# A transformer block in float32: input tiles of the feed forward turned in PSUM banks of their own, and a new order of exponentials, rounding, normalising and splitting in cross attention

## The reference

```
x = x + cross_attention(layernorm(x), ctx)    # 16 heads, queries against a latent context of 257 x 128 per batch
x = x + self_attention(layernorm(x))          # 16 heads of 32
x = x + feed_forward(layernorm(x))
# cross attention, folded, for each batch b (scores of 512 rows = 16 heads x 32 queries):
#   attn = softmax(q_b @ kv_b.T); ctx_c = attn @ kv_b; out = ctx_c through per-head weights
# feed forward:
amp = sigmoid(x @ amp_w + amp_b)
ph  = tanh(x @ ph_w + ph_b) * pi
h   = (cos(ph) + sin(ph)) * amp
for l in range(2):
    h = layer_norm(h + (h @ ent_w[l] + ent_b[l]) @ ent_pw[l] + ent_pb[l], ln3_g[l], ln3_b[l])
    t = einsum('bsd,pdf->pbsf', h, path_w[l]) + path_b[l]
    h = layer_norm(h + sum_p(t * (cos(phase[l]) + sin(phase[l]))), ln4_g[l], ln4_b[l])
```

## Time and profile before

| | |
|---|---|
| median of 3 runs | 1646.76 us (1643.83 to 1646.97) |
| profiled execution | 1646.83 us, its span 1644.8 us |
| mean granted clock of TensorE | 0.956 of full speed |
| cross attention, 600 to 900 us | PE busy 97%, DVE 80%, ACT 53%, POOL 51% |
| feed forward, 1421.8 to 1503.3 us (one turn) | PE busy 94%, DVE 57%, ACT 51%, POOL 25% |

### The profile page before, as it was taken

The page is one execution under the profiler, slowest core; times in us unless marked ns, Lnnn a source line. Parts: engine busy times, 40 slices in busy tenths (PEclk is TensorE's granted clock), DMA queues, the critical chain, the costliest instruction groups (busy, mean ns, idle before and its releaser), DMA issues. The chain is left out here.

```text
span 1644.8 us, 26366 instructions
## 1 busy us (share of the span) xinstructions
PE 1490.0 (91%) x8136; PEld 1129.7 (69%) x8136; DVE 1124.7 (68%) x1815; ACT 809.7 (49%) x1723; POOL 539.5 (33%) x593
## 2 busy tenths in 40 slices
PE   4799999999946999999999987999799499898998
PEld 3577777777635777777777766888444278777876
DVE  6788778887526878787878753777558535555556
ACT  4566665566434555555555533555201355545554
POOL 4235324341024554545454513221051331402021
PEclk9899999999977999999999997999899699999999
DMA  4123334324257544454454414000354000000000
GB/s 152 64 90 95 105 107 127 100 84 114 82 174 242 123 115 116 106 124 109 122 108 116 132 27 168 0 0 1 128 204 154 0 1 1 1 27 0 26 26 26
DMA packets 140505, 143.77 MB, mean 87 GB/s; under 512 B 83488, under 2 KB 103072, under 8 KB 138784
## 3 DMA queue, kind: packets, MB, share of 16 engines
q1 hardware_dynamic: 138720, 133.87, 28.2%
q10 hardware_dynamic: 1728, 9.20, 1.7%
HBM read 113.54 MB, written 29.49 MB: 87 GB/s over the span
## 5 line engine op out<-in xcount | busy, mean ns | idle before, releaser
L942 ACT ACTIVATE c_e_t_high<-c_et_ps 128x512 fp32r<-128x512 f32 x128 | 76.7, 599 | 227.4 <-PE c_et_ps L1011 227.4
L820 POOL TENSOR_TENSOR c_mixed_low<-c_whole,c_mixed_high 128x512 fp32r<-128x512 f32 x64 | 96.0, 1500 | 177.1 <-ACT c_mixed_high L954 177.1
L77 DVE TENSOR_TENSOR b_rot_parts_low<-b_rot,b_rot_parts_high 128x1536 fp32r<-128x1536 f32 x64 | 136.0, 2125 | 21.9 <-ACT b_rot_parts_high L526 21.9
L1003 PE MATMUL c_sc_ps<-c_kv_t,c_q 128*128 128x257 f32 x512 | 136.6, 391 | 13.7 <-DMA c_q<-carried_queries 13.7
L843 DVE TENSOR_REDUCE c_peak<-c_sc_ps 128x2 f32<-128x514 f32 x128 | 88.5, 692 | 55.0 <-PE c_sc_ps L1003 54.3
L264 POOL TENSOR_TENSOR b_turned_raw<-b_turn_part 128x384 f32<-128x384 f32 x32 | 70.1, 2189 | 167.7 <-DVE b_key_parts_low L77 166.5
L1003 PEld LDWEIGHTS c_sc_ps<-c_kv_t,c_q 128*128 128x128 f32 x512 | 99.6, 196 | 33.1 <-DMA c_q<-carried_queries 14.6
L309 DVE TENSOR_TENSOR b_rot<-b_w_qr,b_angle 128x1536 f32<-128x1536 f32 x64 | 119.2, 1863 | 0.2
L1515 PE MATMUL f_ps<-f_right,f_left 128*128 128x512 f32 x256 | 112.5, 601 | 7.3 <-POOL spare L1487 5.0
L934 ACT ACTIVATE c_e<-c_sc_ps,c_peak 128x257 f32<-128x257 f32 x256 | 118.8, 475 | 0.0
L70 PE MATMUL c_out_ps<-c_w_vo_high,c_mixed_high 128*128 128x512 f32 x256 | 112.0, 437 | 3.3 <-POOL c_mixed_low L820 3.3
(11 more groups left out here) (211 smaller groups left out, 3876.3 us busy)
## 6 DMA issues: line engine op xcount, KB each, us to landing
c_q<-carried_queries SPq DMA_DIRECT2D x64, 256.0 KB, 3.7
c_ends_spread<-end_weights SPq DMA_DIRECT2D x64, 256.0 KB, 4.3
carried_queries<-x SPq DMA_DIRECT2D x7, 2048.0 KB, 11.2
b_early<-early SPq DMA_DIRECT2D x15, 640.0 KB, 3.9
c_raw<-cache_t SPq DMA_DIRECT2D x64, 128.5 KB, 3.8
c_swapped<-cache_t SPq DMA_DIRECT2D x128, 64.2 KB, 3.8
f_left<-ent_in SPq DMA_DIRECT2D x16, 512.0 KB, 5.5
f_right<-ent_out SPq DMA_DIRECT2D x16, 512.0 KB, 6.7
```

The costliest lines, as they stand in the source:

```text
L77: return nc.vector.tensor_tensor(low, value, high.bitcast(F32), ALU.subtract)
L820: nc.gpsimd.tensor_tensor(mixed[1][:, w, :, u], whole[:, u % 2].rearrange("p (h s) -> p h s", h=H), mixed[0][:, w, :, u].bitcast(F32), ALU ...
L1003: last = nc.tensor.matmul(sc_ps[:, 2 * half + c, 0:L], q[:, u, at], kv_t[:, u], start=True, stop=True)
```

## The change

In cross attention ACT's `exponential(n+1)` goes ahead of `round_turned(n)`, and DVE's `normalise(n+1)` ahead of `split_turned(n)`, `split_kv` and `add_out`. In feed forward the input tiles get two PSUM banks of their own, `e_input_ps`. They are turned one at a time behind the products of units 3 to 6, and copied and split at the head of units 4 to 7. A turn into a bank waits for the split of the use before it, two tiles back.

```diff
@@ cross attention, VectorE, tile
                         add_end(i - (u == 0), (u - 1) % BT)
+                    if more:
+                        normalise(n + 1, 1 - half)
                     split_turned(n, u, half)
                     if half == 0:
                         split_kv(b, u)
                     if j == 2 and known(i, 2):
                         add_out(i - 2)
-                    if more:
-                        normalise(n + 1, 1 - half)
@@ cross attention, ScalarE, tile
-                    round_turned(n, b, u, half)
                     if not (isinstance(n, int) and n == PAIRS - 1):
                         exponential(n + 1, 1 - half)
+                    round_turned(n, b, u, half)
@@ feed forward
         turn_ps = ctx.enter_context(nc.psum_tensor("e_turn_ps", [P, 2, D], F32))
+        input_ps = ctx.enter_context(nc.psum_tensor("e_input_ps", [P, 2, D], F32))
...
-        next_inputs = {0: (0, 1), 1: (2, 3)}
-        taken_inputs = {1: (0, 1), 2: (2, 3)}
+        next_inputs = {3 + u: (u,) for u in range(G)}
+        taken_inputs = {4 + u: (u,) for u in range(G)}
@@ turn_input
-                if u >= 2:
-                    pe.wait_ge(x_split, t - 1)
-                elif later(i):
-                    if isinstance(i, int) and i == 1:
-                        pe.wait_ge(x_split, G - 1 + u)
-                    else:
-                        pe.wait_ge(y_split, MM * (i - 1) - 1 + u)
+                wait(pe, x_split, t - 1)
                 for c in range(CD):
-                    last = nc.tensor.transpose(turn_ps[:, u % 2, ...
+                    last = nc.tensor.transpose(input_ps[:, u % 2, ...
@@ turn_y (its argument final is gone)
-                if q >= 2:
-                    pe.wait_ge(y_split, MM * i + q - 1)
-                elif final:
-                    pe.wait_ge(y_split, MM * i + q - 1)
-                else:
-                    pe.wait_ge(x_split, G * (i + 1) + G + q - 1)
+                wait(pe, y_split, MM * i + q - 1)
```

More of the change, by code:

```diff
@@ L1733, in turn_input @@
                 pe.wait_ge(normed, t + 1)
-                if u >= 2:
-                    pe.wait_ge(x_split, t - 1)
-                elif later(i):
-                    if isinstance(i, int) and i == 1:
-                        pe.wait_ge(x_split, G - 1 + u)
-                    else:
-                        pe.wait_ge(y_split, MM * (i - 1) - 1 + u)
+                wait(pe, x_split, t - 1)
                 for c in range(CD):
-                    last = nc.tensor.transpose(turn_ps[:, u % 2, c * P:(c + 1) * P], xn[:, u, c * P:(c + 1) * P], ident[:])
+                    last = nc.tensor.transpose(input_ps[:, u % 2, c * P:(c + 1) * P], xn[:, u, c * P:(c + 1) * P], ident[:])
                 last.then_inc(x_turned, 1)
@@ L1777, in multiply, with turn_y @@
                 last.then_inc(multiplied, 1)
-            def turn_y(i, q, final):
+            def turn_y(i, q):
                 pe.wait_ge(y_normed, UNITS * i + q + 1)
-                if q >= 2:
-                    pe.wait_ge(y_split, MM * i + q - 1)
-                elif final:
-                    pe.wait_ge(y_split, MM * i + q - 1)
-                else:
-                    pe.wait_ge(x_split, G * (i + 1) + G + q - 1)
+                wait(pe, y_split, MM * i + q - 1)
                 for c in range(CD):
@@ L1801, in body @@
                             if r < 2:
-                                turn_y(i, MM - 2 + r, final)
+                                turn_y(i, MM - 2 + r)
                     multiply(i, q, final)
@@ L1807, in body @@
                     if 2 <= q < (MM + 2 if final else MM):
-                        turn_y(i, q - 2, final)
+                        turn_y(i, q - 2)
             repeat_to_last(pe, TURNS, body)
@@ L1819, in round_input @@
                     wait(act, gated, 2 * CD * i)
-                nc.scalar.activation(tile_of(xn_t[0], u), turn_ps[:, u % 2].rearrange("p (c x) -> p c x", c=CD), ACT.Copy).then_inc(x_turned_out, 1)
+                nc.scalar.activation(tile_of(xn_t[0], u), input_ps[:, u % 2].rearrange("p (c x) -> p c x", c=CD), ACT.Copy).then_inc(x_turned_out, 1)
             def make_gates(i):
@@ L1891, in split_input @@
                 dve.wait_ge(x_turned_out, G * i + u + 1)
-                low_part(nc, tile_of(xn_t[1], u), turn_ps[:, u % 2].rearrange("p (c x) -> p c x", c=CD), tile_of(xn_t[0], u)).then_inc(x_split, 1)
+                low_part(nc, tile_of(xn_t[1], u), input_ps[:, u % 2].rearrange("p (c x) -> p c x", c=CD), tile_of(xn_t[0], u)).then_inc(x_split, 1)
             def apply_gates(i):
```

## The result

The kernel after takes 1636.82 us (median of 6 runs, 1634.87 to 1638.67) beside 1647.23 us for the kernel before (6 runs, 1643.83 to 1650.47): a ratio of 0.9933, interval 0.9918 to 0.9949, or 10.4 us less. The forecast was 1632.5 us, 14.3 less. The direction came as said. The mechanism did too, but for the start of feed forward's third turn. Both terms of the sum were too large, by some 2 to 3 us each.

The account below looks back on a forecast made before the run. PE (91% busy) was taken as the bound, standing before cross attention's half-1 turn and at feed forward's turn starts. 1646.8 less 7 (cross attention) less 7.3 (feed forward) gave 1632.5 us, range 1622 to 1644.

Parts of the forecast that it names:

- Cross attention, forecast -7: Cross attention: new chain of 7.18 us, 7.76 with the output's addition; 0.11 us saved on each of 60 batches.
- The first tile "at nothing": Cross attention's first tile, without projection: same chain with transfer waits beside it, so no saving was counted.
- Feed forward, forecast -7.3: Feed forward: moving input tiles to later units and own banks saves 7.3 us over three turns, bounds -11 and -2.
- Input units 3.78: Feed forward units with an input tile: bound by DVE and ACT at 3.78 us, 0.54 over 3.24.
- Second turn -3.7: Feed forward's second turn: saves 3.7 us, from 2 to 5, partly because POOL has nothing to do at the start.
- First turn -1.2: Feed forward's first turn: no rows added, PE the bound after the change; saves 1.2 us, from 0 to 2.4.
- Third turn -2.4: Feed forward's third turn: starts like the last turn, with three more inputs; saves 1.9 to 3.2 us, 2.4 taken.
- Cross attention giving nothing: Rival: bare half-0 exponentials on DVE cost what the earlier start saves in cross attention; total 1639.5 us, chance 0.18.
- feed forward giving nothing: Rival: feed forward's input units cost as much as the turn starts give back; total 1639.8 us, chance 0.09.
- The slower one: Rival: POOL's rotation delays cross attention's half-1 normalisation up to 0.7 us; +0.2 a batch, total 1652.5, chance 0.10.
- The floor rival: Rival: cross attention's PE runs without holes, batches fall to about 6.9 us; total 1605 us, chance 0.05.
- What would show it: Signs: batches 7.2 and 7.7, half-0 hole 0.4 released by the split, DVE idle 1.1, input units about 3.8 us.

Follow-up runs that it names:

- act_first: Kernel before with only ScalarE's reordering in cross attention (exponentials ahead of rounding), VectorE's order as before: 1725.98 us, ratio 1.0486.
- dve_first: Kernel before with only VectorE's reordering in cross attention (normalising ahead of splitting), ScalarE's order as before: 1674.9 us, ratio 1.0186.
- ca_only: Kernel before with both cross attention reorderings and feed forward as before: 1641.81 us, ratio 0.9974.
- late_shift: Kernel after, with GpSimd's row shift in the last two feed forward turns waiting until 6 tiles are normalised: 1633.47 us, ratio 0.9923.
- ff_only: Kernel before with the feed forward edits alone (own banks, new places), cross attention as before: 1641.72 us, ratio 0.9975.
- banks_only: Kernel before with input tiles in two banks of their own but at their old places, cross attention as before: 1644.78 us, ratio 1.0001.
- early_late: Kernel after with cross attention's score taken one step earlier, behind PE's turn, plus the wait of late_shift: 1621.22 us, ratio 0.9845.
- short_rotation: early_late with GpSimd's three rotation operations on only 16 of 257 columns from the second tile on: 1611.94 us, ratio 0.9796.
- rotation_apart: early_late with the output's addition ahead of normalising, its last product a step earlier, and GpSimd's rotation split around the normalisations: 1609.31 us, ratio 0.9764.

## Why the prediction was right or wrong

**What bounds the kernel: right.** The hole ahead of the half-1 turn went when the two operations in front of the normalisation went, and not with one of them (`act_first`, `dve_first`).

**Cross attention, forecast -7, measured -5.2 in the trace up to feed forward, -4.5 of it in the batches, and -3.4 in `ca_only`.** The chain came as summed. From the rows of the kernel after: turn to next score 2.56 (2.55 forecast), score to peak 1.30 (1.30), peak to exponential 0.73 (0.73), exponentials to reciprocal 1.05 (1.06), reciprocal to split 0.81 (0.81), split to turn 703.33 to 704.13 = 0.80 (0.73). The sum is 7.25, measured 7.26, forecast 7.18. The mis-sized term is the last: 0.12 us pass from the end of VectorE's split to PE's weight load (704.01 to 704.13; 711.82 to 711.94 in the next batch), where I had put 0.05. In the kernel before 0.05 us lay between the end of the normalisation (708.32, 0.69 long) and the same load at 709.06. Why the split's end takes longer to reach PE is open. With the batch that adds the output at 7.80 for 7.76, the mean gain falls from 0.11 to 0.065 us. On 60 batches that is 3.9 and not 6.9 us.

**The first tile "at nothing": neither shown nor refuted.** From the sixth `add_end` to the last the kernel after takes 427.64 us and the kernel before 432.13, 4.5 less, and the other profiles of either order agree: 427.90 (`ca_only`) and 427.62 (`late_shift`) against 431.55 (`ff_only`) and 432.11 (`banks_only`). The rest of the 5.2 is not to be read as an effect. The sixth `add_end` came 1.15 us later than before (538.94 and 537.79), and from the last one to feed forward 1.9 us were saved (370.06 and 371.97). But from the first peak to the sixth `add_end` the old order takes 62.9, 63.6 and 64.1 us in the same profiles and the new one 64.0, 63.6 and 64.0. From the last `add_end` to feed forward it is 372.0, 370.4 and 369.3 in the old order, 370.1, 369.9 and 370.3 in the new one. Cross attention's first peak itself, behind code that no edit touched, comes anywhere from 473.7 (`banks_only`) to 477.4 us (`late_shift`). One profile of each kernel can't tell an opening's loss or a gain behind the stage.

**Feed forward, forecast -7.3, measured -4.3 in the trace and -3.5 in `ff_only`.** Step by step:
- *Input units 3.78: right.* VectorE's `take` (L1906) starts at 1510.20, 1513.98, 1517.76, 1521.54 and 1525.33: 3.78 us each. No transpose pair stands 4.12 us any more.
- *Second turn -3.7: right* (-3.3, and 3.7 between the shorter kinds). The reason given fits: with GpSimd idle the second to fourth row additions take 0.69, 0.68 and 0.68 us, before 0.79, 1.13 and 1.08, and the normalisations between them 0.55, before 1.35 and 1.59. How much of the 3.3 us this gave beside the gap of 4.12 was not tried.
- *First turn -1.2: too large by a little*, 0.7 to 1.0 like with like; it varies by 1.2 to 1.6 us between executions, with the granted clock of its first 5 us.
- *Third turn -2.4: the step that failed* (-0.3, and 1.0 between the shorter kinds). "Up to 1.3 if the first row addition still collides with POOL" saw one collision. There were three, with an addition of 1.64, one of 1.82 and a normalisation of 1.53 us, because `shift_rows` now runs where VectorE has no time to spare. `late_shift` gives 2.85 us back with one wait, and then the saving is 3.2, the upper end of the forecast's 1.9 to 3.2. "Not needed until q = 12 or the next turn: nothing" was true of the deadline and wrong of the start: in the turn without tiles to normalise POOL came no later at all (the shift starts 3.42 us into the turn in both kernels).
- *Last turn as before: right* (59.52 after 59.47).

**The rivals.** Cross attention giving nothing is refuted by `ca_only`, whose interval excludes 1, and feed forward giving nothing by `ff_only`. The slower one had the right mechanism and the wrong place. The rotation falls beside the normalisation in the half-0 step (706.11, 0.69 there; 0.73 to 0.94 in the other batches of a tile), and what it added was absorbed there, as the rival said of 0.3 us: every ordinary batch of the kernel after has the same 7.26. I gave it 0.7 us at most; 0.25 came. Once the chain is shorter it stands on it (`early_late` against `short_rotation`, 9.3 us). By the rule of the Trainium skill ("SBUF — State Buffer", Who interferes with whom) a VectorE instruction with two SBUF inputs and a GpSimd instruction that reads SBUF exclude each other. The traces agree: a normalisation that issues second ends 0.54 or 0.55 us after GpSimd's operation (703.18 after 702.63; 709.73 after 709.19; 730.28 after 729.73). The floor rival's 6.80 us of PE time was a sound figure, since two later kernels (`short_rotation`, `rotation_apart`) reach 6.80 to 6.82 in a batch. But this change by itself stays at 7.26.

**What would show it** was right on the batches (7.26 and 7.80 for 7.2 and 7.7), the hole of some 0.4 (0.45), VectorE's 1.1 us of idle time (1.09) and the input units. The releaser was right too: the split ends 0.12 us before the load, after the normalisation, and the matmuls' row names it. Only the weight loads' row doesn't: it has 33 of the 43 holes under "issue" and 10 under the normalisation.

## What to carry to other kernels

Where two engines hand a tile to and fro, move the operation that the bound waits for ahead on both at once, then sum the new chain from start to start, signalling included: here 0.07 us of it on 60 batches is some 4 us. When work is moved off a queue, look at what stands behind it on that queue and what runs beside it when it comes early, in every turn by itself, the one without the work above all. A GpSimd operation near a VectorE product with two SBUF inputs can be worth ordering behind it by a wait, even if it is needed by nobody: two such placements gave 6 and 8 us here, where the change gave 10. Before a stage's gain is read from two profiles, compare stretches that no edit touched: here they differ by up to 4 us.

## What the runs showed of the hardware

- The exclusion of VectorE and GpSimd falls on the second to issue: the first keeps its time alone, and starts 0.01 us apart suffice (729.10 and 729.11). The same two operations take 0.69 and 0.98 us, or 1.17 and 0.63. VectorE's product ended 0.54 or 0.55 us behind GpSimd's end in each case, 0.14 less than its 0.69 alone.
- A `TENSOR_SCALAR` with one SBUF input, 0.55 us alone, took 1.53 beside `shift_rows`. It is held back too.
- The same work had two clocks. In the 10 us ahead of feed forward's first turn PE worked 7.86 us at a clock of 1.00 in the kernel after and 7.85 in `ff_only`, and then the first 5 us of the turn had 0.72 in the one and 1.00 in the other. The same holds for the kernel before (0.72) and `banks_only` (1.00).
- The longer hole costs clock as well. In the 5 us behind PE's hole it was 0.66 after 2.28 us (second turn of the kernel after, third of `late_shift`) and 0.50 after 4.39 us (third turn of the kernel after). In executions with the shorter first turn it was 1.00 after 2.28 us (third turn of `early_late`) and 0.66 after 4.40 us (third of `ff_only`). The third turn's difference is 2.85 us for 2.11 us of hole in the one kind (81.08 and 78.23), and 2.63 for 2.12 in the other (80.35 and 77.72).
